# The first tile of step one searched with five rounds on VectorE and no probes on ScalarE

## The reference, cut to what matters

```python
for s in range(STEPS):                       # 2 steps
    A = _adj_from_feats(Xa, W1, W2, W3)      # keep the top 0.9 of each softmax row
    Xf = Rf @ Xf; Xb = Rb @ Xb; Xa = A @ Xa
    Z = Z + (Xf @ U1[s] + Xb @ U2[s] + Xa @ U3[s])
Y = X + Z
```

## Time and profile before

| | us |
|---|---|
| median of 3 runs | 2296.23 |
| lowest and highest | 2295.15, 2298.56 |
| the profiled execution, its own time | 2297.46 |
| its span, first to last instruction | 2295.7 |
| step one's search, first search of tile 0 to that of tile 25 | 75.33 to 877.68 |

### The profile page before, as it was taken

How to read it: one execution, slowest core, us unless ns; L and a number is a source line. 1 busy time by engine, 2 the same in 40 slices (tenths; PEclk the granted TensorE clock), 3 DMA queues, 4 the chain that set the end, 5 groups by cost and what they waited for, 6 DMA issues and landing times.

```text
span 2295.7 us, 26397 instructions
## 1 busy us (share of the span) xinstructions
PE 2140.1 (93%) x8282; PEld 1381.0 (60%) x8282; DVE 2042.6 (89%) x3758; ACT 1935.1 (84%) x2831; POOL 854.2 (37%) x1233
## 2 busy tenths in 40 slices
PE   7599999999999998998899999999999999999987
PEld 4377777777777777543355555555555555555556
DVE  5699999999999998138859999999999999999996
ACT  5899999999999996258379989989989999899844
POOL 2134443344334442003224444444444444444420
PEclk9699999999999999999999999999999999999998
DMA  7255544554455543332322112112212212122242
GB/s 247 79 124 138 113 98 112 129 115 110 101 124 129 114 100 72 105 99 42 54 56 57 39 52 57 44 48 57 52 40 56 52 42 54 52 44 52 54 124 72
DMA packets 85168, 190.05 MB, mean 83 GB/s; under 512 B 12193, under 2 KB 65056, under 8 KB 85024
## 3 DMA queue, kind: packets, MB, share of 16 engines
q0 software_dynamic: 26208, 61.37, 17.1%
q1 hardware_dynamic: 56496, 125.48, 16.5%
q10 hardware_dynamic: 2320, 1.48, 0.2%
HBM read 154.19 MB, written 34.10 MB: 82 GB/s over the span
## 4 chain that ended last, share of the span: by engine, by line
DVE 45%; PE 4%; issue 1%; POOL 0%; ACT 0%; DVEq 0%; ACTq 0%; POOLq 0%
DVE junk L1928 19%; DVE small L1975 4%; DVE logits L1967 4%; DVE logits L2117 4%; DVE small L1871 4%; PE bank L1118 2%; DVE small L1956 1%; DVE small L1959 1%; PE bank L777 1%; DVE small L1980 1%; DVE small L1983 1%; DVE QT L2031 1%; PE bank L1181 1%; PE bank L1144 0%; PE bank L1100 0%
## 5 line engine op out<-in xcount | busy, mean ns | idle before, releaser
L1928 DVE SCALAR_TENSOR_TENSOR junk<-logits,small,expd 128x3327 uint8<-128x3327 f32 x184 | 677.9, 3684 | 4.7
L1144 PE MATMUL bank<-h_aug,turns 128*128 128x256 f32 x2704 | 628.2, 379 | 0.0
L1118 PE MATMUL bank<-both,pair 128*128 128x512 f32 x1352 | 611.2, 596 | 17.8 <-ACT sides L1497 17.8
L1144 PEld LDWEIGHTS bank<-h_aug,turns 128*128 128x128 f32 x2704 | 498.4, 190 | 94.5 <-issue 30.1
L1118 PEld LDWEIGHTS bank<-both,pair 128*128 128x128 f32 x1352 | 251.0, 190 | 302.6 <-issue 261.0
L1118 PE MATMUL bank<-h_aug,both 128*128 128x257 f32 x1352 | 316.6, 384 | 2.8 <-ACT sides L1480 1.6
L1118 PEld LDWEIGHTS bank<-h_aug,both 128*128 128x128 f32 x1352 | 250.9, 190 | 64.5 <-issue 26.9
L1100 PE MATMUL bank<-KTr,QT 64*128 64x512 f32 (+1 forms) x728 | 246.5, 613 | 43.7 <-ACT logits L1344 39.8
L1404 ACT ACTIVATE junk<-expd,small 128x3327 int8<-128x3327 f32 x88 | 270.1, 3069 | 1.5
L1410 ACT ACTIVATE junk<-expd,small 128x3327 int8<-128x3327 f32 x88 | 270.5, 3073 | 0.3
L1473 ACT ACTIVATE turns<-bank 128x512 f32<-128x512 f32 (+1 forms) x364 | 188.7, 562 | 52.0 <-PE bank L1134 46.5
(11 more groups left out here) (263 smaller groups left out, 3097.8 us busy)
## 6 DMA issues: line engine op xcount, KB each, us to landing
both<-adj_turned SPq DMA_DIRECT2D x52, 832.0 KB, 6.8
both<-adj_turned POOLq DMA_DIRECT2D x52, 832.0 KB, 9.3
pair<-adj_turned SPq DMA_DIRECT2D x52, 832.0 KB, 4.5
z<-sides POOLq DMA_DIRECT2D x78, 128.0 KB, 3.2
spread<-sides POOLq DMA_DIRECT2D x26, 128.5 KB, 3.6
turns<-spread SPq DMA_DIRECT2D x26, 128.5 KB, 2.1
attended<-att_out SPq DMA_DIRECT2D x26, 128.0 KB, 8.5
expd<-attended SPq DMA_DIRECT2D x26, 128.0 KB, 2.1
```

Of the source, the lines that this page charges most:

```text
L1118: done = pe.matmul(SX[:, 0:width], half(t, h)[:, bass.ts(jj, P)], rows_of(j), start=(j == 0), stop=(j == T - 1))
L1144: last = pe.matmul(AB[:, 0:D], attT[i % 4][:, b, :], h_aug[:, g + b, 0:D], start=(g + b == 0), stop=(g + b == T - 1))
L1928: chain.did(dve.scalar_tensor_tensor(junk[:, 0:N], logits[t % 3][:, 0:N], col(t, "cand"), expd[t % NE][:, 0:N], ALU.is_gt, ALU.mult, accum ...
```

## The change

It concerns only step one, and in it tiles 0 and 1. ScalarE no longer probes for tile 0; it raises `searched_early` right behind the guess. VectorE starts tile 0's search from the unprobed guess, with the wider step widths, and makes `early + late` = 5 rounds. The step widths for five rounds are ten more constants in a table of 32 columns, set by ten more memsets. TensorE interleaves tile 1's logits with tile 0's adjacency product: chunks 0 to 2 behind the first group, chunk 3 behind the third, chunks 4 to 6 behind the fourth; the weight product comes last. ScalarE copies tile 1's logits right behind the guess of tile 0, and `store_weights` moves behind the exponentials and the guess of tile 1.

```diff
+                def rounds(t):
+                    return early + late if first_step and t == 0 else late
+                def probes(t):
+                    return early + late - rounds(t)
+                def shares(t):
+                    at = 4 if rounds(t) == late else 16
+                    return constants[:, at:at + 2 * rounds(t)]
...
                         if t == 0:
-                            for n in range(NG):
+                            spread(0, 0)
+                            make_logits(1, (0, 1, 2))
+                            spread(0, 1)
+                            spread(0, 2)
+                            make_logits(1, (3,))
+                            spread(0, 3)
+                            make_logits(1, range(4, NC))
+                            for n in range(4, NG):
                                 spread(0, n)
                             last_weights()
-                            make_logits(1, range(NC))
...
                         exponentials(0)
                         guess(0)
-                        for k in range(early):
-                            probe(0, k, nothing, nothing)
+                        act.sem_inc(sem["searched_early"], 1)
...
                         if first_step:
-                            if t == 0:
-                                store_weights()
                             if following:
                                 store_logits(t + 1, range(copied))
...
                                 exponentials(t + 1)
                                 guess(t + 1)
+                                if t == 0:
+                                    store_weights()
                                 probe(t + 1, 0, lambda: turned(0, 1, 2), lambda: turned(3, 4))
...
-                            chain.did(dve.tensor_scalar(col(t, "cand"), pair(t, f"point{early}", 0), col(t, "max"),
+                            chain.did(dve.tensor_scalar(col(t, "cand"), pair(t, f"point{probes(t)}", 0), col(t, "max"),
                                                         LN2 + 3e-5, ALU.add, ALU.add))
-                            spans(t, col(t, "low"), -0.5 ** early)
+                            spans(t, col(t, "low"), -0.5 ** probes(t))
...
-                            for k in range(1, late):
+                            for k in range(1, rounds(t)):
                                 bisect(t, k)
```

More of the change, by code:

```diff
@@ L893, in step @@
                 NA = 2 if first_step else 1
-                constants = sbt("constants", [P, 16])
+                constants = sbt("constants", [P, 32 if first_step else 16])
                 ones = sbt("ones", [P, BEST])
@@ L920, in mask @@
                     return masks[t % 3][:, :]
+                def rounds(t):
[5 more added lines that the diff above has]
+                    return constants[:, at:at + 2 * rounds(t)]
                 def steps_of(t, k=None):
-                    return small[t % 3][:, 72:72 + 2 * late] if k is None else small[t % 3][:, 72 + k:73 + k]
+                    return small[t % 3][:, 72:72 + 2 * rounds(t)] if k is None else small[t % 3][:, 72 + k:73 + k]
                 def best(t, n):
@@ L1880, in spans @@
                     def spans(t, width, halved):
-                        chain.did(dve.tensor_scalar(steps_of(t), constants[:, 4:4 + 2 * late], width, halved,
+                        chain.did(dve.tensor_scalar(steps_of(t), shares(t), width, halved,
                                                     ALU.mult, ALU.mult))
@@ L1952, in bisect @@
                         n = k if first_step else k - 1
-                        last = k == late - 1
+                        last = k == rounds(t) - 1
                         if k == 1 and not first_step:
@@ L1959, in bisect @@
                         chain.did(dve.scalar_tensor_tensor(col(t, "cand"), col(t, "move"),
-                                                           0.0 if last else steps_of(t, late + n),
+                                                           0.0 if last else steps_of(t, rounds(t) + n),
                                                            col(t, "cand"), ALU.add, ALU.add))
@@ L2121, in vector @@
                         dve.memset(constants[:, n:n + 1], value).then_inc(sem["constants_set"], 1)
-                    for n in range(late):
-                        dve.memset(constants[:, 4 + n:5 + n], 0.5 ** (n + 1)).then_inc(sem["setup"], 1)
-                        dve.memset(constants[:, 4 + late + n:5 + late + n], -0.5 ** (n + 2)).then_inc(sem["setup"], 1)
+                    for tile in range(2 if first_step else 1):
+                        for n in range(rounds(tile)):
+                            for at, share in ((n, 0.5 ** (n + 1)), (rounds(tile) + n, -0.5 ** (n + 2))):
+                                dve.memset(shares(tile)[:, at:at + 1], share).then_inc(sem["setup"], 1)
                     dve.memset(constants[:, 0:1], 0.0).then_inc(sem["constants_set"], 1)
@@ L2132, in vector @@
                             dve.memset(logits[i][:, N:NP], 0.0).then_inc(sem["setup"], 1)
-                    dve.wait_ge(sem["setup"], 2 * late + 1 + (NE + 6 if first_step else 0))
+                    dve.wait_ge(sem["setup"], 2 * late + 1 + (NE + 6 + 2 * rounds(0) if first_step else 0))
                     def slot(t):
```

## The result

The changed kernel takes 2287.8 us (median of 7 runs, 2287.14 to 2290.59) against 2296.23 (2295.15 to 2298.56). The ratio is 0.9964, with a 95% interval of 0.9955 to 0.9973: 8.4 us faster. The profiled execution took 2287.14 us at a span of 2285.3, against 2297.46 and 2295.7.

The account below looks back on a forecast made before the run. VectorE's instructions were taken to pace step one, after a start-up wait for ScalarE's probes. -15.83 + 8.56 - 0.99 - 0.22 = -8.48 us, with +0.1 for TensorE, gave 2287.8 us against the 2296.23 median; range 2284.8 to 2293.2.

Parts of the forecast that it names:

- TensorE's slack: TensorE's work up to tile 3's logits may end as late as 129.3: 3.3 us to spare, 2.2 used.
- Start of tile 0's search: On VectorE, tile 0's search begins at 59.50 instead of 75.33, 15.83 us earlier, once GpSimd's `prepared` is there.
- Two rounds: Two more rounds of tile 0 on VectorE cost 4.28 us each, 8.56 us, fully on its path.
- The waits of 0.99 and 0.22 us: VectorE's waits for tile 1's early search (0.99 us) and for tile 2's logits (0.22 us) both go away.
- Tile 1's logits: ScalarE has tile 1's chunks 0 to 3 copied by about 61.5, 2.7 us ahead of VectorE's need at 64.18.
- ScalarE's search of tile 1: ScalarE raises tile 1's `searched_early` at 89.0, 7.1 us ahead of VectorE, without waiting for the weight product.
- Rival B: VectorE's rounds lock out GpSimd's `prepare(1)`, delaying tile 1's search; 3.1 us of gain left, 2293.1 us; chance 0.05.
- The gap and its clock: New TensorE idle of 5 to 6 us ahead of tile 0's transposes, clock at half in it; return costs 2.2 us.
- Between the steps: After step one nothing is gained or lost: 0, with 3 us either way from where half clock falls.
- Rival C: Another engine paces a later tile or the turn to step two, catching over half the 8.4 us: 2292 to 2296; chance 0.07.
- D: Tile 1's logits come late behind the adjacency load; with it 5 us late, 2.3 us lost, 2290.1 us; chance 0.03.
- Rival A: TensorE's clock stays at half behind `keep(0)`, losing 13.5 us: 2301.3 us, slower than before; chance 0.03.

Follow-up runs that it names:

- four-round kernel: Changed kernel with tile 0's last halving left out, four rounds instead of five: 2283.15 us, against 2288.20 for the changed kernel on the same chip.
- taken-early: Changed kernel, but VectorE copies all seven chunks of tile 1's logits itself while waiting, ScalarE none: 2286.65 us against 2297.81 for the kernel before.
- TensorE's old order: Changed kernel, but TensorE makes tile 1's logits behind tile 0's whole adjacency product and the weight product: 2295.11 us against 2296.80 for the kernel before.
- the filled gap: Changed kernel with 9 unread matmul calls in TensorE's gap ahead of tile 0's transposes: 2287.37 us against 2296.54 before; with 18 calls, 2288.72 against 2298.19.
- the repeats: Changed kernel with tile 3's first logits matmul made two or ten times more: 2290.22 and 2295.94 us, against 2298.19 for the kernel before.
- the orders alone: Kernel before with only the new TensorE and ScalarE orders, tile 0 keeping two probes and three rounds: 2299.07 us against 2296.80.

## Why the prediction was right

It said 2287.8 us, and that was measured. The way was right: a start 15.8 us earlier, two rounds more, one wait less, and step one shifted as a whole. That it came out to the tenth is luck. The runs of one kernel spread over some 3 us, and inside step one three small things that the prediction misread or didn't know of (the idle of 0.22 us, TensorE's slack and a pause of 0.47 us, below) shift the gain between 8.24 us at search 3 and 8.72 at search 25. The steps, one by one, in us; times that stand alone are on the changed kernel's profile:

- *Start of tile 0's search.* Forecast 15.83 us earlier, measured 15.76. That GpSimd's `prepared`, not the guess, comes last was right: the wait of 4.37 us ends with L1732.
- *Two rounds.* Forecast 28.04 + 8.56 = 36.60 us from search 0 to search 1, measured 36.53. The four-round kernel gave 4.30 us for one, by removal.
- *The waits of 0.99 and 0.22 us* went away, and search 2 came 8.50 us earlier, forecast 8.48. Only the first of them for the reason given. The prediction read the 0.22 us as a wait for logits that comes with a late ScalarE, but the logits had been there for 1.4 us. An idle of 0.21 us stands ahead of a row maximum in the four-round kernel too (at 160.60, behind search 3) and in the taken-early one (at 226.17, behind search 5), with the logits copied 2.7 us before. Here there is none, which that argument did not foresee; the cause is open.
- *Tile 1's logits.* Copied 2.4 us ahead of need, forecast 2.7. TensorE's old order showed that this was no side matter: without it 7.5 us are lost.
- *ScalarE's search of tile 1.* At 89.4, forecast 89.0. The copy of the weights did wait, 0.26 us, where no wait was forecast, and it was hidden behind the 6.8 us by which ScalarE was ahead (forecast 7.1).
- *Rival B* did not occur. `prepare(1)`'s first operation took 0.37 us, as in the same position before. What can hold GpSimd is seen one tile later, in the changed kernel's timeline of GpSimd: an operation of `prepare(2)` that begins 0.25 us behind the start of VectorE's pass at 109.27 takes 3.50 us, until the pass is over. With the lock of the shared port pair in the Trainium skill ("SBUF — State Buffer", section "SBUF: two separate sides") the trace agrees.

```profile
109.52 3.50 POOL L1725 TENSOR_SCALAR small<-small 128x1 f32<-128x1 f32 x1
```

- *TensorE's slack was wrong.* The step that failed is "Tile 3's logits are wanted at 128.31 + 4.68 = 132.99, and making and copying them takes some 3.7 us, so TensorE may end as late as 129.3", and with it the 3.3 us to spare. It took the consumer with the latest need, VectorE. The one that mattered is ScalarE, which is free at 128.3 and has the tie count, the lift, the attended rows and the exponentials of tile 3 queued behind those copies. TensorE ended at 127.93, 18.52 us behind the transposes' start where 16.80 is its full-clock time: 1.7 us, forecast 2.2. ScalarE's copies came 0.86 us late, forecast 0.5, and the cost to VectorE was 0.2 to 0.27 us (the filled gap), forecast 0.1 of a range of 0 to 2. Any further lateness passed one to one (the repeats). So about 1 us (1.24 less 0.2 to 0.27, by the filled gap) or 1.5 (1.7 less the same, by the full-clock time) was to spare, not 3.3; it made little difference here, because the delay itself was small.
- *The gap and its clock.* The prediction's sign was a gap of 5 to 6 us with the clock at half in it. The gap was 4.49 us and the clock in it 1.00. It was shorter because TensorE's work ahead of it took 14.57 us (90.34 to 104.91), forecast 13.65: the clock came back in the microsecond from 96, some 6 us behind the restart, where it was 4.4 in the kernel before. The half clock stood behind the gap, for about 3.4 us, and the price of one return came out near the forecast all the same.
- *After that*, the shift is 8.24 us at search 3 and 8.72 at search 25. The 0.48 us between are one pause of VectorE in the kernel before, with no other engine named, at the same place in both its profiles:

```profile
532.96 3.68 DVE L2117 SCALAR_TENSOR_TENSOR logits<-logits,small,expd 128x3328 f32<-128x3328 f32 x1 [0.47 <-DVE small L2114]
```

Neither profile of the changed kernel has it, so it is part of what was measured as gain, but no step of the prediction brings it. From search 3 to 25 both profiles of before take 708.7 us, as do the four-round and the taken-early kernel, which also have such a pause of 0.46 us; the other ten profiles take 708.2 to 708.3 and have none. The four profiles with the pause are those with the idle of 0.2 us, some 424 us ahead of it. The two go together; what makes them is open.

- *Between the steps* the forecast was 0, 3 us either way, from the clock. The clock was the right place to look: the first pair of profiles gained 3.15 us there, the second 0.8, and the fourteen profiles sort by their time at half clock. The medians differ by 8.4 and 8.6 us, so over several runs little of it is left. What decides how much half clock an execution gets is open.

Rival C, that something catches the gain later in step one, falls with search 25, where the whole gain is still there. For D there was no sign: the adjacency product began at 52.72, within 0.2 us of where it did before. Rival A fell with the clock: it came back in the microsecond from 113, and from search 3 to 25 it is 1.00.

## What to carry to other kernels

When the start-up of a pipeline leaves the pacing engine idle, work that another engine does better in steady state can be cheaper there, at the price of 8.5 us of rounds for 15.8 us of start; but it needs the next tile's data brought forward in the same step, in the order of each queue, or the wait only moves (7.5 of 8.5 us at search 2 were lost without it, and the orders alone made search 2 come 4.2 us later). Take an engine's slack from the consumer that queues the most behind the data, not from the one that needs it last. When a view names the waiting engine itself as what ended an idle, look whether the data had been there before calling it a wait for data. And count to a fixed point inside the kernel: starts that repeat within 0.06 us decide questions that totals with a scatter of 2 to 4 us can't.

## What the runs showed of the hardware

- Half clock can come behind a gap instead of in it. In the changed kernel's first profile the clock was still 1.00 in the microsecond from 108, and 0.53 in the one from 110, when TensorE had been busy again since 109.41; it came back in the microsecond from 113. In its second profile, with a gap of 4.64 us that ended at 108.82, it fell within the microsecond of the restart (0.87 in the row below). In the kernel before, it fell within an idle stretch. Waits of 3.21 to 3.32 us near 950 had half clock in three profiles, one of 3.03 us in a fourth had none. The Trainium skill, page "TensorE: Matmul & The Clock Gate", section "What's actually happening", says that the gate's window is free-running and doesn't start anew with a kernel; that the fall stands at a different place from one profile of the same kernel to the next agrees.

```profile
108.00:109.00 1.00, 0.18 (x1) 0.87 0.96 186
```

- From search 25 to the first search of step two, an execution with no half clock took 172.3 to 173.0 us, one with 3.4 us of it 173.5 to 174.5, one with 6.8 us 175.1 to 176.1.
- An fp32 matmul call is two instructions on TensorE: 18 calls of 128x256 were 36 instructions and 7.93 us, 0.22 us each. A repeat of a 64x512 logits call cost 0.86 us.
